# Expert slots of a routed feed-forward layer: the normalised rows made one slot further ahead in three buffers, and two register loads moved behind relu

## What is computed

```python
x = x + xattn(layernorm(x), ctx, ctx, mask, Wq, bq, Wk, bk, Wv, bv, Wo, bo)   # 16 heads of 8
x = x + ffn(layernorm(x), Wr, br, ln_g, ln_b, W1, b1, W2, b2)

def ffn(x, Wr, br, ln_g, ln_b, W1, b1, W2, b2):      # E = 8 experts, D = 128, F = 512
    probs = softmax(x @ Wr + br)
    gate, idx = max(probs), argmax(probs)
    xn = (x - mean(x)) / sqrt(var(x) + 1e-5) * ln_g + ln_b
    h = relu(xn @ W1[idx] + b1[idx])
    return (h @ W2[idx] + b2[idx]) * gate
```

## Time and profile before

| | |
|---|---|
| median of three runs | 397.69 us (395.61 to 399.92) |
| the profiled execution, its own time | 394.74 us |
| its span, first to last instruction | 393.0 us |
| busy in the span | PE 303.1 us (77%), DVE 304.9 us (78%), ACT 202.0 us (51%), POOL 163.5 us (42%) |
| mean granted TensorE clock | 0.850 of full speed |
| span of the experts' stage | from about 283.7 us (first G load) to the end |

### The profile page before, as it was taken

One profiled execution on the slowest core, in us unless ns is written; L12 is line 12 of the kernel. 1 busy time (PEld: TensorE's weight loads), 2 busy tenths in 40 slices (PEclk: granted clock), 3 DMA queues, 4 the chain that ended last, 5 costly groups with the idle time before them and its releaser, 6 DMA issues.

```text
span 393.0 us, 10023 instructions
## 1 busy us (share of the span) xinstructions
PE 303.1 (77%) x3066; PEld 240.2 (61%) x3066; DVE 304.9 (78%) x1159; ACT 202.0 (51%) x548; POOL 163.5 (42%) x220
## 2 busy tenths in 40 slices
PE   0449888788998878877798988963079898978990
PEld 0327656556875655654585776762078887867880
DVE  1247899999989999999999999756747776767771
ACT  1127666466456555646546465511056666656650
POOL 3314445455435545545544543333104443434442
PEclk9999989978568997999968595555569999999997
DMA  5955543234325333424324324000011112112110
GB/s 127 416 132 145 147 137 104 84 111 136 87 85 155 93 90 107 136 84 139 110 85 133 89 84 125 10 14 14 16 42 43 54 54 61 42 50 64 54 32 3
DMA packets 58228, 36.31 MB, mean 92 GB/s; under 512 B 5295, under 2 KB 56116, under 8 KB 58176
## 3 DMA queue, kind: packets, MB, share of 16 engines
q1 hardware_dynamic: 54592, 31.30, 27.5%
q0 software_dynamic: 2272, 4.27, 3.3%
q10 hardware_dynamic: 1312, 0.11, 0.5%
HBM read 14.03 MB, written 22.09 MB: 92 GB/s over the span
## 4 chain that ended last, share of the span: by engine, by line
issue 37%; DVE 31%; POOL 15%; DMA 6%; PE 5%; DVEq 2%; ACTq 1%; POOLq 1%; SPq 0%; ACT 0%
POOL rows_dram L355 5%; DVE Pr L539 3%; DVE mx L535 3%; POOL rs L333 3%; POOL row L343 3%; DMA out<-ot,G 3%; DVE hT L660 3%; DVE xt L500 3%; DVE xh L648 3%; DVE ot L669 2%; POOL xb L338 2%; POOL Kb L348 2%; DMA G<-rows_dram 2%; DVE yb L667 2%; DMA Wr<-in_wr 1%
## 5 line engine op out<-in xcount | busy, mean ns | idle before, releaser
L366 POOL DMA_INDIRECT out<-ot,G x39 | 39.8, 1020 | 67.8 <-DVE ot L669 66.7
L343 POOL TENSOR_TENSOR row<-ve,half 128x2 f32<-128x2 f32 x32 | 24.7, 771 | 103.1 <-DVE ve L589 103.1
L413 ACT ACTIVATE Pr<-Pr,rowany 128x1024 f32<-128x1024 f32 x32 | 36.7, 1148 | 59.8 <-DVE Pr L539 59.8
L706 PE MATMUL ps<-ident,Pr 128*128 128x128 f32 x256 | 51.2, 335 | 0.1
L396 ACT ACTIVATE PT<-ps 128x512 f32<-128x512 f32 x64 | 38.2, 597 | 18.4 <-PE ps L706 17.6
L706 PEld LDWEIGHTS ps<-ident,Pr 128*128 128x128 f32 x256 | 37.0, 173 | 16.8 <-issue 9.1
L796 PE MATMUL ps<-xg,WR 128*128 128x128 f32 x312 | 45.5, 291 | 0.0
L752 PE MATMUL ps<-VB,PT 128*64 128x18 f32 x1024 | 42.1, 228 | 0.3 <-ACT GT L403 0.3
L535 DVE TENSOR_REDUCE mx<-ps 128x16 f32<-128x1024 f32 x32 | 38.9, 1216 | 3.3 <-PE ps L695 3.3
L807 PE MATMUL ps<-WR,hT 128*128 128x128 f32 x312 | 41.2, 276 | 0.0
L796 PEld LDWEIGHTS ps<-xg,WR 128*128 128x128 f32 x312 | 39.5, 199 | 1.4
(11 more groups left out here) (113 smaller groups left out, 633.8 us busy)
## 6 DMA issues: line engine op xcount, KB each, us to landing
rows_dram<-empty SPq DMA_DIRECT2D x32, 528.0 KB, 4.4
WA<-in_wpk SPq DMA_DIRECT2D x8, 578.0 KB, 9.2
G<-rows_dram SPq DMA_DIRECT2D x39, 66.0 KB, 1.9
X<-in_x SPq DMA_DIRECT2D x32, 64.0 KB, 4.1
C<-in_ctxT SPq DMA_DIRECT2D x32, 64.0 KB, 1.8
Cv<-in_ctxT SPq DMA_DIRECT2D x32, 64.0 KB, 2.0
out<-ot,G POOLq DMA_INDIRECT x39, 2.3
rows_dram<-row,posi POOLq DMA_INDIRECT x32, 2.5
```

Of the source, the lines that this page charges most:

```text
L366: g.indirect_dma_start(out=out, out_offset=bass.IndirectOffsetOnAxis(ap=G[:, q, D + 2:D + 3].bitcast(I32), axis=0), in_=ot[:, q, :], in_of ...
L413: a.activation(Pr[:, q, :], Pr[:, q, :], ACT.Exp, scale=rowany[:, 0:1]).then_inc(s_p, 1)
L706: last = nc.tensor.transpose(ps[:, 4 + m, 128 * j:128 * j + 128], Pr[:, q, 128 * (4 * m + j):128 * (4 * m + j) + 128], ident[:])
```

## The change

Three edits, all in the experts' stage. xh gets three buffers. On VectorE norm(t) is called for slot s + 3 behind relu of slot s, where it was called for slot s + 2 ahead of it, and a third norm stands before the loop; G keeps its six buffers. The register loads of both engines, which stood directly ahead of the copy that uses them, stand behind relu: on VectorE ahead of norm, on ScalarE ahead of xg.

```diff
-        xh = sb("xh", [P, 2, P])
+        xh = sb("xh", [P, 3, P])
...
-            def stage_w1(s):
-                ex = act.value_load(slot[0:1, 0, s:s + 1], min_val=0, max_val=E - 1)
+            def stage_w1(s, ex):
                 wait(act, b_up, s - NW + 1)
...
             for s in range(-2, SLOTS):
+                if s + 2 < SLOTS:
+                    ex = act.value_load(slot[0:1, 0, s + 2:s + 3], min_val=0, max_val=E - 1)
                 if 0 <= s + 1 < SLOTS:
...
-                    stage_w1(s + 2)
+                    stage_w1(s + 2, ex)
...
-            def stage_w2(s):
-                ex = dve.value_load(slot[0:1, 0, s:s + 1], min_val=0, max_val=E - 1)
+            def expert_of(s):
+                return dve.value_load(slot[0:1, 0, s:s + 1], min_val=0, max_val=E - 1)
+
+            def stage_w2(s, ex):
...
             def norm(t):
                 q = t % R
                 dve.wait_ge(g_in[q], 16 * (t // R + 1))
-                wait(dve, b_tx, t - 1)
-                v.tensor_scalar(xh[:, t % 2, :], G[:, q, 0:D], G[:, q, D + 1:D + 2], G[:, q, D:D + 1],
+                wait(dve, b_tx, t - 2)
+                v.tensor_scalar(xh[:, t % 3, :], G[:, q, 0:D], G[:, q, D + 1:D + 2], G[:, q, D:D + 1],
                                 ALU.mult, ALU.add).then_inc(b_xh, 1)
 
             norm(0)
             norm(1)
+            norm(2)
             for s in range(SLOTS + 1):
                 if s < SLOTS:
                     dve.wait_ge(b_up, s + 1)
-                    if s + 2 < SLOTS:
-                        norm(s + 2)
                     wait(dve, b_dn, s - 1)
                     for c in range(NA, FC):
                         v.tensor_scalar(hT[:, s % 2, P * c:P * c + P], h_ps(s, c), b1_of(s, c), 0.0,
                                         ALU.add, ALU.max).then_inc(b_rd, 1)
+                    if s + 2 < SLOTS:
+                        ex = expert_of(s + 2)
+                    if s + 3 < SLOTS:
+                        norm(s + 3)
                 if s >= 1:
...
-                    stage_w2(s + 2)
+                    stage_w2(s + 2, ex)
...
-                    nc.tensor.transpose(ps[:, 4 + t % 2, 0:P], xh[:, t % 2, :], ident[:]).then_inc(b_tx, 1)
+                    nc.tensor.transpose(ps[:, 4 + t % 2, 0:P], xh[:, t % 3, :], ident[:]).then_inc(b_tx, 1)
```

More of the change, by code:

```diff
@@ L640, in stage_w2 @@
                 v.tensor_copy(WR[:, s % NW:s % NW + 1, F:WP], WA[:, bass.ds(ex, 1), F:WP]).then_inc(b_w2, 1)
-            stage_w2(0)
-            stage_w2(1)
+            stage_w2(0, expert_of(0))
+            stage_w2(1, expert_of(1))
             def norm(t):
```

## The result

The changed kernel takes 415.47 us (median of four runs, 411.64 to 418.55), the kernel before 398.81 (395.61 to 402.26): the ratio is 1.041, 95% interval 1.027 to 1.056. The profiled execution took 413.61 us with a span of 411.9, where before it was 394.74 and 393.0. Medians are of all runs; a ratio with its interval compares only the runs of the faster of the two states in which these programs execute, and is missing where a kernel had too few of them. The two traces differ by 18.9 us, and I read where these are.

What follows compares the result with a forecast made beforehand. The prediction saw VectorE's own work and the scatter and load of G taking turns as the bound in the experts' stage. Slots 20.8, late landings 4.4, register load -1.0 sum to 24.2; 397.69 + 24.2 = 422 us, range 412 to 432.

Steps and rivals of the forecast that it cites:

- The mechanism: Experts' stage: six buffers of G with xh(s + 3) ahead of ot(s - 1) leave two slots, not three, to cover scatter and load.
- the turn-around: Experts' stage: time from the end of ot(t - 6) to the start of xh(t), through scatter and load of G; 5.29 us.
- The slot: Experts' stage: 3.11 us a slot instead of 2.48, paid 33 times by slots 6 to 38, 20.8 us more.
- L: The turn-around: end of ot(t - 6) to start of xh(t), put at 5.29 us from the profile before the change.
- The late landings: Three scatters landing 1.8, 2.0 and 0.7 us over the median would delay the stage; priced 2.2 to 4.4, taken as 4.4.
- The sum: Whole kernel: 20.8 + 4.4 - 1.0 = 24.2 us more, 422 us on the median.
- The register load on VectorE: Ahead of xh it costs 0 to 0.48 us, covered by the wait for G; without that wait, the whole gain.
- The -1.0 us for the iterations outside the ring: VectorE's moved register load saves time only in the first three and last three iterations, 6 x 0 to 0.48 us.
- The rival "faster than before": xh(s + 3) finds its rows, the register load leaves VectorE's path, TensorE's 2.22 us a slot bound: 389 us; chance 0.03.
- The rule on a lighter memory load: Slower slots load memory less, so scatters and loads of G land faster: 2.96 us a slot, 412 us; chance 0.06.
- TensorE's clock: Clock falls to 1.2 GHz in the experts' stage: 430 us for a third of slots, 444 for all; chances 0.17, 0.03.

## Why the prediction was right

**The mechanism** held in each step: six buffers with xh(s + 3) ahead of ot(s - 1) leave two slots for the turn-around; 31 of 33 xh wait for G; the chain is scatter, load, ot; scatters come in pairs. Taking the ring's hold away (eight buffers) takes the loss away, and taking a buffer from the kernel before brings a like one. This is shown by runs, not only by the trace.

**The slot** was put at 3.11 us with L = 5.29; measured are 3.06, with L = 5.26 in the mean of the waiting rows: 0.80 to the scatter's start, 2.54 to the load's issue and 1.92 to xh, where the prediction had 0.79, 2.51 and 1.99. The 20.8 us of this term came to 98.06 - 79.25 = 18.8. The prediction counted 33 waits; the first of them, 2.79 us ahead of slot 6, cost nothing, since xh started there no later than before.

**The late landings** are the term that was mis-sized: 4.4 us taken, none of it paid to scatters. The scatters of the changed kernel landed in at most 2.9 us (line L366, 297 to 400 us):

```profile
DMA to landing us min/median/max: 2.1/2.3/2.9
```

The two over 4 us of the earlier trace rows have no counterpart there. This line can leave landings out (with only the loads moved it gives a maximum of 3.1, beside the 4.04 of the chain shown above), but SP's issues bear it out here: the longest from a scatter's start to the load that waits for it is 3.28 us. Four loads were late instead: slots 16, 30, 37 and 38 began xh 2.34 to 2.89 us after the issue, where 1.9 is usual. What they are over the usual, 2.3 us together, is inside the 3.06.

There is an order in the late ones that the prediction did not see. In several of these traces they lie seven slots apart: the scatters of slots 13 and 20 before, and again with eight buffers; 12 and 19 in the change with eight buffers; 24 and 31 with only the loads moved; the loads of slots 9, 16 and 23 with only xh moved, and of 30 and 37 in the change. What makes them is open.

**The sum.** With the scatters' term at nothing and 18.8 for the slots, 24.2 falls to about 18, and the profiles differ by 18.9. On the medians it is 16.7, a third less than was forecast; both errors lie on the same side, and the range of 412 to 432 holds 415.47 because it reached well below the 422 of the sum.

**The register load on VectorE** was bounded by 0 and 0.48 ahead of xh. One row has 0.11 (above); in the change with eight buffers, 27 xh did not wait, and they start between 0.10 us before relu's end and 0.14 behind it, 20 of them before it, as neighbouring instructions here do anyway. So it is next to nothing, and VectorE's shortest turn is 1.76 us:

```profile
324.99 0.34 DVE L651 TENSOR_SCALAR xh<-G 128x128 f32<-128x128 f32 x1
...
326.23 0.60 DVE L662 TENSOR_SCALAR hT<-ps,WR 128x128 f32<-128x128 f32 x2
326.75 0.34 DVE L651 TENSOR_SCALAR xh<-G 128x128 f32<-128x128 f32 x1
```

That it would be covered by the wait was right, and that it "would be the whole gain" if the wait were not there too. The -1.0 us for the iterations outside the ring was too much: from the end of the instruction that writes the table slot (282.78 before, 283.32 in the changed kernel) to xh of slot 6 the changed kernel took 0.6 us less, and it lost nearly as much by reaching that point 0.5 us later, in a part that the change does not touch.

**The rival "faster than before"** had its condition right (L under what the ring can cover) and its price wrong. TensorE's floor was taken as its busy time, 2.22 us a slot, and gave 389 us; opened by two more buffers the stage ran at 1.92 and the kernel at 374. Back to back, the three groups of a slot start 0.11, 0.89 and 0.89 us apart, 1.89 in all (rows above). In the earlier trace rows the starts are 0.21, 0.96 and 1.17 apart, and the records (0.33, 1.13 and 1.06 long) still cover all but the last 0.11: even back to back a record runs 0.17 us into the next group (1.06 against 0.89), and where groups stand apart this covers short waits. The floor must be read from starts where the engine never waits.

**The rule on a lighter memory load**, which the prediction takes from the Trainium skill ("DMA: Bandwidth & Descriptors", section "Latency and other measured facts"), did not show here: at 42 GB/s instead of 52 the median scatter stayed at 2.3 us, and L was 5.26 where 5.29 had been worked out. The step in load is small, so this is no test of the rule at large.

**TensorE's clock** fell once, and no wait of VectorE shows a cost of it.

## What to carry to other kernels

Before a consumer is moved earlier in its loop, count how many iterations then lie between the release of a ring's buffer and its next use, against the turn-around of that buffer read from the chain of waits; a ring that is deep enough for one order of the code is too shallow for another, with no line of the ring changed. A wait that can block should stand behind the work that releases the next buffer, not ahead of it. And where a change loses, look in the trace for a stretch in which the new limit does not yet bind: here one iteration at the front, 1.98 us long, hinted at the gain that two more buffers then brought, 5% of the kernel.

## What the runs showed of the hardware

A register load directly behind ot, whose result the next instruction needs, left VectorE idle 0.48 us a slot. Behind relu and ahead of xh it left between nothing and 0.14 us. Put back to the first place, with eight buffers, it made a slot 0.45 us longer (2.37 against 1.92). Why the same load is nearly free behind relu was not separated. One difference between the places is that ot waits for a semaphore that yb, directly ahead of it, raises, and relu has no such neighbour.

The turn-around of a scatter and the load that waits for it is not one number: 5.26, 5.45 and 5.30 us in the mean where two slots cover it, 5.48, 5.77 and 5.88 where three do. It does not go by the spacing of the slots alone (5.48 at 2.14 us, 5.77 at 2.43). Single scatters took over 4 us where the median is 2.3, and single loads over 3 where it is 1.9, often seven slots apart.
